# A paged attention kernel: the first tile's third weight block and its turned queries are placed ahead of VectorE's position and angle work

## What is computed

```python
# layer 0: 32 query heads, 8 key/value heads of 128; 16 pages of 32 cached tokens per sequence
q, k, v = x @ Wq.T, x @ Wk.T, x @ Wv.T
q, k = rope(rmsnorm(q, q_norm_w), pos), rope(rmsnorm(k, k_norm_w), pos)   # pos = cache_seqlens + 0..31
kc = k_cache[block_table].reshape(bsz, 512, HK, D)                       # the same for v_cache
scores = einsum('bqhd,bkhd->bhqk', q, concat(kc, k)) * SCALE             # cached keys beyond the length masked
x = x + einsum('bse,de->bsd', softmax(scores) @ concat(vc, v), Wo)
# layer 1: dense product, plus the two best of eight experts of rank 16
x = x + x @ W.T + 2.0 * einsum('bter,bte,eor->bto', einsum('btd,erd->bter', x, A), gates, B)
```

## Time and profile before

| | |
|---|---|
| median of 3 runs | 1478.95 us (1477.67 to 1482.95) |
| span of the profiled execution | 1451.3 us |
| PE busy | 1356.5 us, 93% of the span |
| DVE busy | 1132.6 us, 78% |
| POOL busy | 973.1 us, 67% |
| ACT busy | 766.9 us, 53% |

### The profile page before, as it was taken

The page is one execution under the profiler, slowest core; times in us unless marked ns, Lnnn a source line. Parts: engine busy times, 40 slices in busy tenths (PEclk is TensorE's granted clock), DMA queues, the critical chain, the costliest instruction groups (busy, mean ns, idle before and its releaser), DMA issues.

```text
span 1451.3 us, 28498 instructions
## 1 busy us (share of the span) xinstructions
PE 1356.5 (93%) x8640; PEld 1162.0 (80%) x8640; DVE 1132.6 (78%) x2891; ACT 766.9 (53%) x1989; POOL 973.1 (67%) x1269
## 2 busy tenths in 40 slices
PE   2599999998999999999999999999999999999889
PEld 1478888887878888887777888888787888888777
DVE  6688877777887778788877878887888888777754
ACT  1356555555664555556554555666555556555431
POOL 5676777777766677776766777777777777676500
PEclk8699999999999999999999999999999999999999
DMA  6434444454543343436533433445544343435401
GB/s 228 133 87 121 133 119 134 123 173 133 173 117 116 125 119 125 135 108 202 164 117 107 138 112 112 128 125 181 170 142 129 104 129 117 131 122 167 124 22 58
DMA packets 61380, 188.72 MB, mean 130 GB/s; under 512 B 10736, under 2 KB 11504, under 8 KB 58608
## 3 DMA queue, kind: packets, MB, share of 16 engines
q0 software_dynamic: 40960, 134.25, 31.3%
q1 hardware_dynamic: 19504, 53.50, 10.5%
q10 hardware_dynamic: 864, 0.46, 0.1%
HBM read 177.95 MB, written 12.32 MB: 131 GB/s over the span
## 4 chain that ended last, share of the span: by engine, by line
PE 69%; DVE 21%; issue 5%; ACT 2%; DMA 1%; DVEq 1%; POOL 0%; SPq 0%; ACTq 0%; POOLq 0%
PE PROJ L182 13%; PE MISC L182 13%; PE O L359 10%; PE S L182 10%; PE PT L349 8%; PE KT L338 5%; DVE probs L736 4%; PE O L361 3%; DVE scores L729 2%; PE PROJ L328 2%; DVE kT_lo L750 2%; DVE rope_v L703 2%; PE PROJ L330 2%; DVE mask L716 2%; DVE rope_u L699 2%
## 5 line engine op out<-in xcount | busy, mean ns | idle before, releaser
L976 POOL DMA_INDIRECT kv_rows<-in_kv,step_idx x512 | 529.8, 1035 | 219.6 <-issue 117.8
L550 ACT ACTIVATE pT<-PT 128x640 f32<-128x640 f32 x256 | 180.2, 704 | 300.6 <-PE PT L349 300.6
L359 PEld LDWEIGHTS O<-pT,kv_rows 128*128 128x128 f32 x2048 | 262.6, 192 | 27.0 <-ACT pT L550 9.8
L359 PE MATMUL O<-pT,kv_rows 128*128 128x128 f32 x2048 | 274.8, 277 | 2.9 <-ACT pT L550 2.6
L546 ACT ACTIVATE kT_hi<-KT 128x512 fp32r<-128x512 f32 x256 | 151.2, 590 | 225.1 <-PE KT L338 225.0
L750 DVE TENSOR_TENSOR kT_lo<-KT,kT_hi 128x512 fp32r<-128x512 f32 x256 | 176.0, 687 | 71.3 <-ACT kT_hi L546 70.7
L554 ACT ACTIVATE probs<-scores,min_all 128x640 f32<-128x640 f32 x256 | 212.7, 831 | 23.3 <-DVE min_all L729 21.0
L349 PEld LDWEIGHTS PT<-ident,probs 128*128 128x128 f32 x1280 | 142.1, 141 | 89.9 <-DVE probs L736 78.7
L349 PE MATMUL PT<-ident,probs 128*128 128x128 f32 x1280 | 191.3, 280 | 22.7 <-DVE probs L736 22.3
L729 DVE CUSTOM_DVE_ANT_0 scores<-S,mask,min_new 128x512 f32<-128x512 f32 x256 | 190.5, 744 | 0.0
L182 PE MATMUL PROJ<-w_hi,x_hi 128*128 128x512 f32 x384 | 172.0, 448 | 15.0 <-DVE w_lo L663 12.6
(11 more groups left out here) (215 smaller groups left out, 2702.6 us busy)
## 6 DMA issues: line engine op xcount, KB each, us to landing
stage<-in_wqkv SPq DMA_DIRECT2D x12, 1024.0 KB, 7.7
x_raw<-in_xT SPq DMA_DIRECT2D x32, 256.0 KB, 4.2
stage<-in_wo SPq DMA_DIRECT2D x8, 1024.0 KB, 6.6
kv_rows<-in_kv,step_idx POOLq DMA_INDIRECT x512, 3.7
y_tile<-y_running SPq DMA_DIRECT2D x32, 256.0 KB, 3.7
y_running<-y_tile SPq DMA_DIRECT2D x31, 256.0 KB, 2.1
out<-kv_rows SPq DMA_DIRECT2D x8, 256.0 KB, 2.0
stage<-in_w1T SPq DMA_DIRECT2D x1, 1024.0 KB, 6.7
```

The costliest lines, as they stand in the source:

```text
L359: nc.tensor.matmul(O[:, 0:P], kv_rows[:, b, c, GK * D + h * D:GK * D + (h + 1) * D], pT[:, c * P:(c + 1) * P], start=c == 0, stop=False)
L550: nc.scalar.activation(pT[:, :], PT[:, 0:KEYS], ACT.Copy).then_inc(sm["pT_ready"], 1)
L976: G.indirect_dma_start(kv_rows[:, b, c, :], None, kv[:, :], bass.IndirectOffsetOnAxis(ap=step_idx[:, b * LC + c:b * LC + c + 1], axis=0)). ...
```

## The change

Both edits are in VectorE's order before step 0.

```diff
             round_weights(w_hi[:, 0, :, :], 0, 1)
             rest_weights(0)
             round_weights(w_hi[:, 1, :, :], 1, 1)
+            dve.wait_ge(sm["w_lo_ready"], 1)
+            round_weights(w_hi[:, 2, :, :], 0, 2)
+            dve.wait_ge(sm["w_lo_ready"], 2)
+            rest_weights(2)
             dve.wait_ge(sm["consts_in"], 80)
...
             angles(slice(0, 1))
-            dve.wait_ge(sm["w_lo_ready"], 1)
-            round_weights(w_hi[:, 2, :, :], 0, 2)
-            dve.wait_ge(sm["w_lo_ready"], 2)
-            rest_weights(2)
             dve.wait_ge(sm["trig"], 2)
             rotate(0, 0)
             rotate(0, 1)
             rest_kT(0, 0)
-            angles(slice(1, TILES), (0,))
             rotate(0, 2)
-            angles(slice(1, TILES), (1,))
             rest_kT_new(0)
             for h in range(GK):
                 rest_qT(0, h)
+            angles(slice(1, TILES), (0, 1))
             dve.wait_ge(sm["trig"], 4)
```

## The result

| | before | changed |
|---|---|---|
| median of 12 runs each, us | 1478.93 | 1481.26 |
| lowest and highest | 1474.43, 1484.88 | 1477.46, 1486.57 |
| ratio (95% interval) | | 1.0029 (1.0015 to 1.0043) |
| profiled execution: span, own time | 1451.3, not listed | 1477.6, 1479.55 |

By the recorded ratio the change costs 4.3 us (2.2 to 6.4), which is 0.3%: by the bound of 0.5% it counts as no difference, and its sign is slower. This ratio is not that of the two medians, which lie 2.3 us apart (the means 3.0); both lie in its interval. Forecast were 1482.0 us and +3.0.

A forecast was written before the change was run, and what follows sets the result against it. TensorE was taken as busy nearly throughout, so the change could move only the start. Projection +2.55 and clock +0.45 made +3.0 us: span 1454.3, with the carried 27.65 a time of 1482.0 us, range 1476.0 to 1488.5.

The forecast's parts named there:

- angles: VectorE's 17 angle operations for tiles 1 to 7, behind the query rest: together 9.2 us, hidden only by TensorE's new scores.
- projection: TensorE's projection of the next tile, waiting for VectorE's reductions: starts at 67.2 instead of 64.66, +2.55 us.
- rival (e): VectorE's third-block cast runs at once beside GpSimd: everything 1.2 us earlier, +1.8, 1480.7 us; chance within the forecast's 0.75.
- Begins near 19.35: Sign in VectorE's timeline: the third block's cast begins near 19.35 us, once GpSimd's subtraction is done.
- The clock's term: TensorE after its idle stretch: about two more matmuls at the low clock, some 0.22 us each, +0.45 us (0 to 0.9).
- GpSimd's +2.6: GpSimd's tables at 34.7 instead of 32.09 us: row numbers 5.2 late, less 2.6 from gather issues no longer stretched.
- I leave that distance as it is: The 27.65 us between the profiled span, 1451.3, and the median, 1478.95, carried over unchanged to reach 1482.0 us.
- Rival (a): Row 0's gather still lands late, towards 47.0 us, sharing DMA engines with the copy: +9.3, 1488.2 us; chance 0.07.
- Rival (b): GpSimd's long gather issue is not relieved: GpSimd 1.85 us later throughout, sum +4.85, 1483.8 us; chance 0.10.
- Rival (c): Turned queries come no earlier, query rest stays at 59.04: TensorE +6.9, with the clock +7.4, 1486.3 us; chance 0.05.
- (d): The landing's 5.2 us gain comes through whole, with the angles covered by VectorE idle time: 1473.8 us; chance 0.03.
- The check that the distance from projection to end be the same within 1 us: Sign for the later tiles: their rhythm stays unchanged; otherwise the prediction is wrong in the large.

The follow-up runs named there:

- e3: Kernel before, with only the copy of x into y_running held until row 0's gathers have landed; -3.1 us (-4.9 to -1.5) against the kernel before.
- e8: Kernel before, start rebuilt: third block's cast on ScalarE, second's subtraction on VectorE, copy after row 0, row 1 gathered later, angles split; 1445.97 us beside 1453.0.
- e4: Changed kernel without the 17 angle operations of tiles 1 to 7 (sines and cosines zeroed, output not valid); -4.7 us (-6.4 to -3.1) against the kernel before.
- e6: Changed kernel with nine angle operations ahead of the third rotation, memset, mask and x split right behind it, eight behind the query rests; -2.3 us against the kernel before.
- e2: Kernel before, with all 17 angle operations moved behind the query rests and the third block's split left late; +6.7 us (4.1 to 9.2) against the kernel before.
- e9: Changed kernel, unaltered, run again on a third chip; 1478.23 us, +1.9 us (-0.4 to 4.1) against the kernel before.
- e12: Changed kernel with ten extra TensorE products, results unused, between the new scores and first score product; 1479.49 us, +2.4 us (0.0 to 4.9) against the kernel before.
- e1: Kernel before, with only the third block's split moved early and the angles in their old places; -0.7 us (-3.0 to 1.5) against the kernel before.
- e11: e8 with its nine angle operations moved ahead of the third rotation; 1470.11 us, -7.4 us (-10.2 to -4.6) against the kernel before.

## Why the prediction was right, step by step

The mechanism held: an earlier landing and earlier queries, given back by the angles, with the shift of the projection carried to the end. The steps, forecast and measured:

| step | forecast | measured |
|---|---|---|
| cast held behind GpSimd; subtraction ends | 22.95 | 22.38 |
| row numbers complete | 28.45 | 27.68 |
| GpSimd's tables | 34.7 | 33.92 |
| landing | 37.4 | 37.56 |
| first query block | 48.2 | 47.46 |
| query rest ends | 54.6 | 54.14 |
| angles | 9.2 | 8.9 |
| reductions end | 67.15 | 66.38 |
| projection | 67.2 (+2.55) | 66.61 (+1.95) |
| clock | +0.45 | +1.48 |
| sum (measured: the second minimum) | +3.0 | +3.4 |

- The times up to the projection are some 0.6 us early, all but the landing. 0.4 of it is that GpSimd began its subtraction at 14.37, not 14.78. The cast began at 17.31, as rival (e) had it, and yet gained nothing from that: it was held until GpSimd was done. "Begins near 19.35" was the wrong thing to look for; its end was the right one.
- **The clock's term was three times too small.** The step said that about two more matmuls would run at the low level. In fact all nine did and the three score products behind them, as rows of 0.63 us show: 0.85 us more from the projection to the scores and 0.63 more from there to the second minimum. It made up for a projection that was 0.6 us earlier than forecast. That the sum is nearer than its terms is luck. The prediction had called GpSimd's +2.6 its weakest term; that one was 0.8 too large (+1.8), the clock's was off by more.
- **"I leave that distance as it is" was wrong reading**, though it did no harm. The 27.65 us between span and median are 2 us around a span and, as far as the spans and steps show, the difference of two chips. The shift could be added to the median only because it does not depend on the chip; a term proportional to the loop would have needed the runs' own chip.
- Rival (a), the late gather, did not happen: the landing came 3.7 us behind the last issue's end, and e3 showed that the copy had been the cause. Rival (b), which the Trainium skill's page "SBUF — State Buffer", section "Who interferes with whom", would have given, is refuted twice: the issues are back at 0.95 us in the changed kernel, and in e8 the subtraction by itself stretches one to 2.22. By that page's statement on descriptors, which it calls inferred, the subtraction should have left the issue alone; the measurement decides. But the same section also says that a VectorE instruction with two SBUF inputs contends with a GpSimd instruction that reads SBUF, and these issues read their row numbers from `step_idx` in SBUF. The prediction left that out. Read so, the page allows the long issue after all, and no run here tells which of the two accesses is held.
- Rival (c) did not happen. For (d) the condition was named rightly: the 5 us come through if the angles are covered. e4 puts that case at -4.7 us.
- The check that the distance from projection to end be the same within 1 us cannot be made where it was asked, between chips. On the quicker ones, for five starts that lie 8 us apart, the distances differ by 2.1 us (1385.2 to 1387.3), 0.8 of it by the low clock (2.53 us from the projection to the scores in e8, 3.29 in e6); from the second minimum they differ by 1.3.

What the prediction did not see is how the two parts of the change hang together: the early split alone gives only 0.7 us, mostly because the cosines hold the queries. It asked what the angles cost behind the queries, not what they cost ahead of them once the queries could be early.

## What to carry to other kernels

Before moving filler work out of a wait, ask on which side it will be on the path: behind the last thing that releases the next engine it costs its whole length, ahead of it only what overhangs the wait and what it takes from an engine beside it. Here 17 operations filled two waits. The first nine fit in theirs with 2.6 us to spare (e6) and cost the 1.1 us by which GpSimd's first query block was late; behind the queries they would cost 4.9. The eight overhung the second wait, and those had to go.

When a transfer lands late, look at which large transfer ends at the same moment before making the issue earlier: one wait ahead of a copy that nobody needed yet was worth 3.1 us here. And compare a span with a time only within one execution.

## What the hardware showed that I had not expected

- Chips run the same kernel 24 to 26 us (1.7 to 1.8%) apart, by 1.1 us in most steps at two ScalarE copies, with landing and first query block alike to 0.3 us.
- The low clock after a pause lasted for 2.9 us of work (e2) and for 5.7 and 6.2 (changed kernel and e9) after the same 6.5 us idle, and a pause of 2.64 us was enough to lose the full clock in e12.
- VectorE operations of 0.39 to 0.69 us take 1.1 to 1.7 beside GpSimd's 128x512 sums (e1, e6, e8, e11), and a gather issue of GpSimd that begins inside a 128x2048 subtraction on VectorE ends 0.8 us behind it (2.80 and 2.22 us instead of 0.95). It goes the other way too: beside VectorE's 448-column operations GpSimd's `rstd` took 1.43 us for 1.05 (e1 and the changed kernel). Each of them made an order that looked free cost a microsecond.
